# Token products one turn further ahead, between z and y, with a second tile for P

## Chip, core and metric

One core of one Trainium2 chip. The metric is the device time in microseconds (us) of one execution, lower is better; the profiled execution also has a span, from its first to its last instruction.

## What is computed

A residual chain of four conditional layers on x (64 batches x 64 rows x 512):

```python
def _L0(x, W_base, Wt, A, B_w, Wp, scaling, e0):       # e0: one of 4 per batch
    base = einsum('bsi,oi->bso', x, W_base)
    h = einsum('bsi,ji->bsj', x, Wt)
    z = einsum('bsj,brj->bsr', h, A[e0])
    l = einsum('bsr,bor->bso', z, B_w[e0])
    return base + einsum('bso,po->bsp', l, Wp) * scaling[e0][:, None, None]
def _L1(x, W, A, Bm, scalings, e1):                    # e1: one of 8
    return einsum('btd,od->bto', x, W) + einsum('btr,bor->bto', einsum('btd,brd->btr', x, A[e1]), Bm[e1]) * scalings[e1][:, None, None]
x = x + _L0(...)
x = x + _L1(...)
x = x + einsum('bct,bcd->bdt', x, w2[e2])              # e2: one of 8, w2 is 64x64
x = x + einsum('bct,bcd->bdt', x, w3[e3])              # e3: one of 200, w3 is 64x64
```

The first two layers mix the 512 columns and the last two mix the 64 rows of a batch, so the order can be changed.

## The kernel before

The set-up (the first 60 us, in part) builds tables from the weights: `g01` = (1 + W_base)(1 + W) as two parts (a high one and the rest), 4 x 8 pairs of low-rank tables, `v_table` in HBM and `u_tab` in SBUF. The batches are taken two at a time (128 rows, a pair), and four pairs are a turn; there are `QUADS` = 8 turns, i = 0 to 7. For turn i:

- **Tokens** (`token_mix`, line 1019 on): P = (1 + w2)(1 + w3) of each of the 8 batches, 64x64. They read `w2_sel`/`w3_now` (filled by VectorE, `place_w2` and `add_w3`) and write banks 1 and 2 of `y_ps`. The trace shows two instructions for each f32 product, so 16 here. ScalarE copies them to `p_now` (`copy_p`, line 507), the only tile for P.
- **y** (`mix`): x times P, 128 instructions of 64x64 into `y_ps`. VectorE copies y to `y_all` (line 733), ScalarE and VectorE split it into a high part and a rest, `yy` (lines 500 and 740).
- **z** (`reduce`): y times the low-rank table u that GpSimd has placed in `u_sel` (`place_u`, line 408), 64 instructions of 128x32 into bank `o_ps[0]`. ScalarE copies z (line 522).
- **v products** (`add_v`): z times the rows that GpSimd has fetched from `v_table` by indirect DMA (`fetch_v`, line 396), 16 instructions into the four banks `o_ps`.
- **Outputs** (`apply`): `yy` times `g01`, 48 products of 512 columns, added in the same banks. ScalarE copies banks 0 and 2 out (line 532), VectorE 1 and 3 (line 780); SyncE stores.

The order on TensorE is written out by hand. A **burst** of turn i holds what isn't an output: tokens of i+1, z of i, y of i+1 (`mix(i + 1, 1)`, `mix(i + 1, 0)`), v products of i; then come the outputs of i. Bursts 2 to 6 run in a loop (`pe.Fori`, line 1176), burst 1 ahead of it, and turn 7 behind it. In `burst`, the function `x_ready` (lines 1105 to 1108) waits ahead of the last of four chunks of z for p_set (P is copied) and for both loads of x. `next_ready` (1084 on) waits ahead of the last output product for y's copies and for w2 and w3. `v_ready` (1064) waits ahead of the v products. Line 872 is the helper that issues each product, so all products carry its number.

The 64x64 tables of layer 3 come in four picks of 16 batches: GpSimd's `pick_w3(g)` (line 387, indirect DMA, into `v_tab`), SyncE's `spill_w3(g)` to HBM and `load_w3(g)` back into `w3_all`. Picks 2 and 3 (turns 4 to 7) are behind `place_u(2, 1)` in GpSimd's queue. GpSimd's queue of turn 1 is `place_u(1, 1)`, then `fetch_v(1)` after the v products of turn 0.

VectorE's order in turn i: last copy out of i-1, rest of y, the four copies of y(i+1), `place_w2(i + 2)`, `add_w3(i + 2)`, then rests and copies out. Each wait of all this is on a semaphore against a count; in the loop these counts are computed from the loop's register by small sequencer instructions (shown as ALU_OP and FUSED_REGOPS), and a wait that no instruction can carry becomes an EVENT_SEMAPHORE.

## Time and profile before

| | |
|---|---|
| median of 3 runs | 167.16 us (167.01 to 167.16) |
| profiled execution | 168.06 us |
| its span | 166.3 us |
| TensorE busy | 161.5 us, 97% |
| VectorE, GpSimd, ScalarE busy | 55%, 35%, 28% |
| DMA | 30.80 MB, mean 185 GB/s |

The profile's page gives, for the profiled execution, each engine's busy time, the span in 40 slices with the clock that TensorE was granted, and the chain of work that ended last. Behind it stands a trace of single instructions, from which timelines of one engine, busy times in chosen stretches, and the instructions of one line or tile can be read. TensorE has two rows: the products, and the loads of their stationary blocks (PEld). Instructions of a sequencer are marked q. Times are from the span's start.

### The profile page before, as it was taken

Reading aid. Unit: us, or ns where it says so; the run is one execution under the profiler, and the core shown is the slowest. Engines: PE = TensorE matmul, PEld = TensorE weight load, DVE = VectorE, ACT = ScalarE, POOL = GpSimd, SP = SyncE. Lnnn points to the kernel's source line nnn. Section 1 sums busy time; section 2 is a strip of 40 time slices with the busy share of each in tenths; the row PEclk is TensorE's granted clock in tenths of the full one; section 3 lists DMA queues with packets and bytes.
Section 4 is the critical chain, followed back from the end, with each engine's and each line's share of the span. In section 5 each row is a group of like instructions: output and inputs, shape, how many; then the busy total and the mean of one; then the engine's idle time right before and its main releaser. Section 6 shows DMA issues by size and latency. Waiting matters only on the chain.

```text
span 166.3 us, 6376 instructions
## 1 busy us (share of the span) xinstructions
PE 161.5 (97%) x2365; PEld 125.6 (75%) x2365; DVE 92.2 (55%) x220; ACT 47.2 (28%) x90; POOL 57.5 (35%) x167
## 2 busy tenths in 40 slices
PE   5999999999999999999999999999999999999993
PEld 5788738767786868886877887788778886887783
DVE  4856865689877394357726843783484345333011
ACT  3135124573215204220322213122402420422110
POOL 4261120354541269227404820490067007500000
PEclk9999999999999999999999999999999999999999
DMA  4899994658844824569834822683076321433113
GB/s 146 267 371 317 275 267 163 174 210 292 285 149 170 282 102 130 187 181 364 280 132 145 313 96 78 215 289 126 7 269 231 126 91 48 119 126 130 65 63 126
DMA packets 21949, 30.80 MB, mean 185 GB/s; under 512 B 7273, under 2 KB 9705, under 8 KB 21929
## 3 DMA queue, kind: packets, MB, share of 16 engines
q1 hardware_dynamic: 20320, 25.31, 45.7%
q0 software_dynamic: 1600, 5.24, 10.1%
q8 instruction: 10, 0.16, 0.4%
q14 instruction: 11, 0.08, 0.2%
q10 hardware_dynamic: 8, 0.00, 0.0%
HBM read 19.80 MB, written 10.75 MB: 184 GB/s over the span
## 4 chain that ended last, share of the span: by engine, by line
PE 97%; POOL 1%; issue 0%; ACT 0%; POOLq 0%
PE o_ps L872 70%; PE y_ps L872 21%; PE o_ps L917 2%; PE y_ps L956 1%; PE y_ps L885 1%; PE y_ps L925 1%; PE y_ps L931 0%; PE y_ps L969 0%; PE y_ps L1000 0%; ACT o_sb L577 0%; POOL ident L376 0%; POOL piece L373 0%; PE y_ps L934 0%; POOL ident L371 0%; POOL owner L374 0%
## 5 line engine op out<-in xcount | busy, mean ns | idle before, releaser
L872 PE MATMUL o_ps<-g,yy 128*128 128x512 f32 (+1 forms) x384 | 89.0, 389 | 0.0
L872 PEld LDWEIGHTS o_ps<-g,yy 128*128 128x128 f32 x384 | 70.5, 188 | 20.3 <-issue 5.3
L408 POOL COPY u_sel<-u_tab 128x64 f32 x128 | 32.4, 273 | 60.6 <-PE o_ps L872 40.1
L740 DVE TENSOR_TENSOR yy<-y_all,yy 128x512 fp32r<-128x512 f32 x32 | 22.2, 698 | 25.6 <-ACT yy L500 25.4
L500 ACT ACTIVATE yy<-y_all 128x512 fp32r<-128x512 f32 x32 | 20.1, 629 | 51.1 <-PE o_ps L872 23.7
L780 DVE COPY o_sb<-o_ps 128x512 f32<-128x512 f32 x15 | 10.4, 691 | 22.0 <-PE o_ps L872 15.4
L733 DVE COPY y_all<-y_ps 128x512 f32<-128x512 f32 x32 | 19.9, 682 | 3.8 <-PE y_ps L872 3.8
L396 POOL DMA_INDIRECT v_sel<-v_table,v_rows x16 | 15.5, 967 | 10.9 <-PE o_ps L872 7.5
L532 ACT ACTIVATE o_sb<-o_ps 128x512 f32<-128x512 f32 x16 | 9.4, 591 | 21.5 <-PE o_ps L872 17.6
L769 DVE COPY w_sel<-w2T 64x64 f32 x56 | 11.4, 215 | 4.8 <-issue 2.3
L872 PE MATMUL o_ps<-g,wb 128*128 128x512 f32 x48 | 13.4, 424 | 0.0
L872 PE MATMUL y_ps<-p_now,x_odd 64*64 64x64 f32 x768 | 12.6, 220 | 0.0
L872 PEld LDWEIGHTS y_ps<-p_now,x_odd 64*64 64x64 f32 x768 | 11.7, 135 | 0.5
L872 PEld LDWEIGHTS o_ps<-g,wb 128*128 128x128 f32 x48 | 9.0, 199 | 2.8 <-issue 0.8
L872 PE MATMUL o_ps<-v_sel,z 32*64 32x512 f32 (+1 forms) x128 | 8.9, 606 | 0.0
L872 PE MATMUL o_ps<-y_all,u_sel 128*32 128x64 f32 x384 | 7.9, 222 | 0.0
L872 PEld LDWEIGHTS o_ps<-y_all,u_sel 128*32 128x32 f32 x384 | 6.2, 109 | 1.1
L507 ACT ACTIVATE p_now<-y_ps 128x256 f32<-128x256 f32 x6 | 2.3, 385 | 13.7 <-PE y_ps L872 13.7
L917 PE MATMUL o_ps<-ident 128*128 128x128 f32 x12 | 3.0, 425 | 2.1 <-POOL ident L376 2.1
L462 ACT ACTIVATE g<-y_ps 128x512 fp32r<-128x512 f32 (+2 forms) x5 | 2.5, 511 | 8.6 <-PE y_ps L925 7.1
L417 POOL TENSOR_TENSOR wb_sb<-wb_sb,ident 128x128 f32<-128x128 f32 x4 | 1.8, 456 | 8.8 <-DMA wb_sb<-in_L_cond_W_base_dram 8.8
L387 POOL DMA_INDIRECT v_tab<-in_L_cond_weights_dram,spread x4 | 4.3, 1076 | 1.4 <-DVE spread L688 0.8
(121 smaller groups left out, 118.5 us busy)
## 6 DMA issues: line engine op xcount, KB each, us to landing
out_dram<-o_sb SPq DMA_DIRECT2D x14, 512.0 KB
x_odd<-in_x_dram SPq DMA_DIRECT2D x12, 512.0 KB
x_even<-in_x_dram SPq DMA_DIRECT2D x4, 512.0 KB
w_sb<-in_L_cond_W_dram SPq DMA_DIRECT2D x4, 256.0 KB, 5.3
wb_sb<-in_L_cond_W_base_dram SPq DMA_DIRECT2D x4, 256.0 KB, 5.8
wp_sb<-in_L_cond_Wp_dram SPq DMA_DIRECT2D x2, 512.0 KB, 7.8
wt_sb<-in_L_cond_Wt_dram SPq DMA_DIRECT2D x1, 1024.0 KB, 9.9
w_of<-v_tab SPq DMA_DIRECT2D x4, 256.0 KB, 3.2
```

The source lines that it names most:

```text
L387: pool.indirect_dma_start(out=w3_pick[:, g, :], out_offset=None, in_=w3_pieces, in_offset=bass.IndirectOffsetOnAxis(ap=w3_rows[:, g, 0:1], ...
L396: pool.indirect_dma_start(out=v_sel[:, h, :], out_offset=None, in_=v_table, in_offset=bass.IndirectOffsetOnAxis(ap=v_rows[:, h, i:i + 1], ...
L408: nc.gpsimd.tensor_copy(u_sel[2 * h + u][:, :, b, RANK * part:RANK * part + RANK], u_tab[:, :, bass.ds(e, 1), :].rearrange("p k a r -> p k ...
L462: nc.scalar.activation(dst, src, ACT.Copy).then_inc(setup_act, 1)
L500: nc.scalar.activation(yy[u][:, :, 0, :], y_all[u][:, :, :], ACT.Copy).then_inc(yh_set, 1)
L532: nc.scalar.activation(o_sb[:, u, :], o_ps[u][:, :], ACT.Copy).then_inc(o_set, 1)
L733: nc.vector.tensor_copy(y_all[u][:, :, :].rearrange("p k (b t) -> p b k t", b=2), y_of(u)).then_inc(yf_set, 1)
L740: nc.vector.tensor_tensor(yy[u][:, :, 1, :], y_all[u][:, :, :], yy[u][:, :, 0, :].bitcast(F32), ALU.subtract).then_inc(yl_set, 1)
L769: nc.vector.tensor_copy(to[rows, u, :], w2T[rows, bass.ds(g, 1), :].rearrange("p a c -> p (a c)")).then_inc(w2_placed, 1)
L780: nc.vector.tensor_copy(o_sb[:, u, :], o_ps[u][:, :]).then_inc(o_set_dve, 1)
L872: return nc.tensor.matmul(dst, lhsT, rhs, start=start, stop=stop)
L917: nc.tensor.transpose(o_ps[3][:, 0:PART], ident[:, :], ident[:, :])
```

## The change

P of turn i+2 is computed in the burst of turn i. Its tokens stand between z(i) and y(i+1), and are written into banks 1 and 2 of `o_ps` (banks 2 and 3 for turn 2, which is done ahead of y of turn 1). P gets a second tile, `p_next`: ScalarE's `take_p(i + 2)` copies the banks to it after z's copy, and `turn_p(i + 2)` copies `p_next` to `p_now` once y(i+1) has read it. `copy_p` is left for turns 0 and 1. The waits for w2 and w3 of the tokens move from `next_ready` into `x_ready`, with two new ones for the copies out of banks 1 and 2; the wait for u moves to `next_ready`; the v products wait for p_next_set. VectorE places w2 and w3 of turn i+3 in turn i. One more turn is taken out of the loops of TensorE, ScalarE and VectorE. Picks 2 and 3 of w3 move ahead of `place_u(1, 1)`, and SyncE's spills ahead of the first store.

```diff
@@ -148,7 +149,8 @@
         y_ps = ctx.enter_context(nc.psum_tensor("y_ps", [PART, QUAD, D], F32))
-        o_ps = [ctx.enter_context(nc.psum_tensor(f"o_ps{n}", [PART, D], F32)) for n in range(QUAD)]
+        o_all = ctx.enter_context(nc.psum_tensor("o_ps", [PART, QUAD, D], F32))
+        o_ps = [o_all[:, n, :] for n in range(QUAD)]
         bank = [y_ps[:, 0, :], y_ps[:, 1, :], y_ps[:, 2, :], o_ps[2][:, :],
@@ -228,6 +231,10 @@
         p_bank = y_ps[:, 1, 0:QUAD * SEQ]
+        def p_banks(i):
+            return y_ps[:, 1:3, :] if isinstance(i, int) and i < 2 else o_all[:, 2:4, :] if isinstance(i, int) and i == 2 else o_all[:, 1:3, :]
         def crossed(i):
@@ -333,12 +340,12 @@
                 load(3, h)
-            store(0, 0)
-            store(0, 1)
             for g in range(2, PICKS):
                 spill_w3(g)
+            store(0, 0)
             for g in range(2, PICKS):
                 load_w3(g)
+            store(0, 1)
             store(1, 0)
@@ -439,18 +446,17 @@
             fetch_v(0)
+            pool.wait_ge(y_done, 2 * QUAD)
+            for g in range(2, PICKS):
+                pick_w3(g)
             pool.wait_ge(z_done, 2)
             place_u(1, 1)
-            pool.wait_ge(y_done, 2 * QUAD)
             fetch_v(1)
...
                 place_u(i + 1, 1)
-                if i == 1:
-                    for g in range(2, PICKS):
-                        pick_w3(g)
         @block.scalar
@@ -503,13 +509,22 @@
                 wait(act, y_done, QUAD * i)
-                if crossed(i):
-                    nc.scalar.activation(p_now[:, :, :].rearrange("p (v w) d -> p w v d", w=2),
-                                         y_ps[:, 1:3, 0:2 * SEQ].rearrange("p w (v d) -> p w v d", d=SEQ),
-                                         ACT.Copy).then_inc(p_set, 1)
-                else:
-                    nc.scalar.activation(p_now[:, :, :], p_bank.rearrange("p (n d) -> p n d", d=SEQ),
-                                         ACT.Copy).then_inc(p_set, 1)
+                nc.scalar.activation(p_now[:, :, :], p_bank.rearrange("p (n d) -> p n d", d=SEQ),
+                                     ACT.Copy).then_inc(p_set, 1)
+            def take_p(i):
+                act.wait_ge(p_done, 2 * QUAD * (i + 1))
+                act.wait_ge(p_set, i)
+                nc.scalar.activation(p_next[:, :, :].rearrange("p (v w) d -> p w v d", w=2),
+                                     p_banks(i)[:, :, 0:2 * SEQ].rearrange("p w (v d) -> p w v d", d=SEQ),
+                                     ACT.Copy).then_inc(p_next_set, 1)
+            def turn_p(i):
+                act.wait_ge(p_next_set, i - 1)
+                act.wait_ge(y_done, QUAD * i)
+                nc.scalar.activation(p_now[:, :, :], p_next[:, :, :], ACT.Copy).then_inc(p_set, 1)
             def copy_half_z(h):
@@ -531,14 +546,16 @@
                 nc.scalar.activation(o_sb[:, u, :], o_ps[u][:, :], ACT.Copy).then_inc(o_set, 1)
-            def turn(i, more=True):
-                if more:
-                    copy_p(i + 1)
+            def turn(i, ahead=True, more=True):
                 high_y(i, 3)
                 copy_z(i, o_ps[0] if more else y_ps[:, 0, :])
+                if ahead:
+                    take_p(i + 2)
                 if more:
...
                     copy_out(i, 0)
+                    if ahead:
+                        turn_p(i + 2)
                     high_y(i + 1, 1)
@@ -562,14 +579,17 @@
             copy_half_z(1)
+            take_p(2)
+            turn_p(2)
             for u in range(3):
...
             turn(1)
-            with act.Fori(2, QUADS - 1) as i:
+            with act.Fori(2, QUADS - 2) as i:
                 turn(i)
-            turn(QUADS - 1, more=False)
+            turn(QUADS - 2, ahead=False)
+            turn(QUADS - 1, ahead=False, more=False)
             copy_out(QUADS - 1, 0, by=2 * QUAD * QUADS)
@@ -742,7 +762,7 @@
             def add_w3(i, to=w3_now):
-                if isinstance(i, int) and i < 4:
+                if isinstance(i, int):
                     dve.wait_ge(w3_in[i // 2], 16)
@@ -786,8 +806,8 @@
                 if ahead:
-                    place_w2(i + 2)
-                    add_w3(i + 2)
+                    place_w2(i + 3)
+                    add_w3(i + 3)
                 if more:
@@ -836,18 +856,22 @@
                 copy_y(0, u)
-            for u in range(2, QUAD):
-                low_y(0, u)
+            low_y(0, 2)
+            add_w3(2)
             place_w2(2)
+            low_y(0, 3)
             for u in (2, 3, 0, 1):
                 copy_y(1, u)
-            add_w3(2)
-            for u in range(3):
+            for u in range(2):
                 low_y(1, u)
+            place_w2(3)
+            add_w3(3)
+            low_y(1, 2)
             copy_out(0, 1, by=2 * QUAD)
             turn(1)
-            with dve.Fori(2, QUADS - 2) as i:
+            with dve.Fori(2, QUADS - 3) as i:
                 turn(i)
+            turn(QUADS - 3, ahead=False)
             turn(QUADS - 2, ahead=False)
@@ -1025,7 +1049,7 @@
                         rows, to = token_rows(i, u, b), slice(SEQ * b, SEQ * b + SEQ)
-                        out_p = (y_ps[to, 1 + u % 2, SEQ * (u // 2):SEQ * (u // 2) + SEQ] if crossed(i)
+                        out_p = (p_banks(i)[to, u % 2, SEQ * (u // 2):SEQ * (u // 2) + SEQ] if crossed(i)
                                  else p_bank[to, SEQ * u:SEQ * u + SEQ])
@@ -1084,7 +1108,7 @@
                 pe.wait_ge(yf_set, QUAD * i + QUAD)
-                token_ready(i + 1)
+                place_ready(i)
             def reduce(bank, h, ready=None):
@@ -1097,21 +1121,27 @@
                 return done
-            def burst(i):
-                token_mix(i + 1)
-                place_ready(i)
+            def burst(i, ahead=True):
                 pe.wait_ge(o_set, 2 * i - 1)
...
                     pe.wait_ge(p_set, i + 2)
+                    if ahead:
+                        token_ready(i + 2)
+                        pe.wait_ge(o_set_dve, 2 * i - 1)
+                        pe.wait_ge(o_set, 2 * i)
                     for h in range(2):
...
                 reduce(o_ps[0], 1, x_ready).then_inc(z_done, 1)
+                if ahead:
+                    token_mix(i + 2)
                 mix(i + 1, 1)
...
                 v_ready(i)
+                if ahead:
+                    pe.wait_ge(p_next_set, i + 1)
                 add_v(0)
@@ -1163,19 +1193,24 @@
             reduce(y_ps[:, 0, :], 1).then_inc(z_done, 1)
+            token_ready(2)
+            token_mix(2)
             mix_ready(1, 1)
...
             mix(1, 0)
+            pe.wait_ge(p_next_set, 1)
             apply(0, 2, first=True)
...
             burst(1)
-            with pe.Fori(1, QUADS - 2) as i:
+            with pe.Fori(1, QUADS - 3) as i:
                 outputs(i, lambda: next_ready(i + 1))
                 burst(i + 1)
+            outputs(QUADS - 3, lambda: next_ready(QUADS - 2))
+            burst(QUADS - 2, ahead=False)
             outputs(QUADS - 2)
```

## Rows read from the trace of the kernel before

**Rows 1.** the page: busy time of the engines; TensorE's granted clock in 40 slices.

```profile
PE 161.5 (97%) x2365; PEld 125.6 (75%) x2365; DVE 92.2 (55%) x220; ACT 47.2 (28%) x90; POOL 57.5 (35%) x167
...
PEclk9999999999999999999999999999999999999999
```

**Rows 2.** the chain that ended last, in order of time: start us, us, what.

```profile
55.71 1.29 PE o_ps L872 x62
...
86.97 0.39 PE y_ps L872 x16
87.36 1.23 PE o_ps L872 x64
88.59 2.02 PE y_ps L872 x128
...
150.14 1.03 PE y_ps L872 x64
```

**Rows 3.** timeline of 102.2 to 107.5, ScalarE: start, duration us, line, out<-in.

```profile
103.43 0.39 ACT L507 ACTIVATE p_now<-y_ps 128x256 f32<-128x256 f32 x1 [2.24 <-PE y_ps L872]
...
104.52 0.28 ACT L522 ACTIVATE z<-o_ps 128x128 f32<-128x128 f32 x1 [0.19 <-PE o_ps L872]
```

**Rows 4.** stretch, its us, busy us (count) of weight loads from u_sel, clock.

```profile
103.86:104.03 0.17, 0.05 (x4) 1.00 0.00 0
```

**Rows 5.** line 1108 in 103 to 105: duration ns min/median/max, starts us.

```profile
L1108 PEldq ALU_OP  x1: 36/36/36, 103.9 to 103.9; - x1
L1108 PEldq EVENT_SEMAPHORE  x1: 51/51/51, 104.0 to 104.0; - x1
```

**Rows 6.** line 1066, then tile x_odd, 74 to 75: columns as in rows 5.

```profile
L1066 PEldq ALU_OP  x1: 32/32/32, 74.4 to 74.4; - x1
...
L872 PE MATMUL y_ps<-p_now,x_odd x36: 218/218/218, 74.1 to 74.6; 64*64 64x64 f32 x36
```

**Rows 7.** timeline of 37 to 62, VectorE.

```profile
43.22 1.36 DVE L740 TENSOR_TENSOR yy<-y_all,yy 128x512 fp32r<-128x512 f32 x2
44.64 1.33 DVE L769 COPY w_sel<-w2T 64x64 f32 x5
46.43 0.77 DVE L769 COPY w_sel<-w2T 64x64 f32 x3 [0.46 <-issue]
...
49.92 0.41 DVE L753 TENSOR_TENSOR w_now<-w_all,ident 128x256 f32<-128x256 f32 x1
...
52.70 0.68 DVE L780 COPY o_sb<-o_ps 128x512 f32<-128x512 f32 x1
```

**Rows 8.** timeline of 39 to 60.2, TensorE.

```profile
46.29 2.10 PE L872 MATMUL y_ps<-p_now,x_odd 64*64 64x64 f32 x128
...
58.95 1.11 PE L872 MATMUL o_ps<-v_sel,z 32*64 32x512 f32 x16
```

**Rows 9.** timeline of 37 to 68, one ScalarE row, then GpSimd.

```profile
52.66 1.09 ACT L532 ACTIVATE o_sb<-o_ps 128x512 f32<-128x512 f32 x2 [0.61 <-PE o_ps L872]
...
53.38 0.97 POOL L396 DMA_INDIRECT v_sel<-v_table,v_rows  x1 [4.18 <-PE o_ps L872]
54.66 0.94 POOL L396 DMA_INDIRECT v_sel<-v_table,v_rows  x1 [0.30 <-issue]
...
61.06 0.97 POOL L396 DMA_INDIRECT v_sel<-v_table,v_rows  x1 [0.44 <-issue]
62.34 1.07 POOL L396 DMA_INDIRECT v_sel<-v_table,v_rows  x1 [0.30 <-issue]
63.41 1.95 POOL L408 COPY u_sel<-u_tab 128x64 f32 x8
...
66.80 1.21 POOL L387 DMA_INDIRECT v_tab<-in_L_cond_weights_dram,spread  x1 [0.30 <-issue]
```

**Rows 10.** line 396, issues in 53 to 56, then in the whole run.

```profile
DMA to landing us min/median/max: 4.0/4.3/4.6
...
DMA to landing us min/median/max: 3.3/3.7/6.2
```

More of the change, by code:

```diff
@@ L139, in build @@
         p_now = sb("p_now", [PART, QUAD, SEQ])
+        p_next = sb("p_next", [PART, QUAD, SEQ])
         w2_sel = sb("w2_sel", [PART, QUAD, SEQ])
@@ L180, in build @@
         p_done, p_set = sem("p_done"), sem("p_set")
+        p_next_set = sem("p_next_set")
         x_even_in = [sem(f"x_even_in{h}") for h in range(2)]
```

## The prediction, made before the change was run

> **What bounds the kernel now.** I read the page's busy shares first, then the chain that ended last, then the stretches in which the order of TensorE's work changes. TensorE is busy 97% of a 166.3 us span, and its clock stands at the upper level (2.4 GHz) in every slice [rows 1]. The chain is TensorE's own instructions from start to end. So a change counts only by what it takes off TensorE's stream or puts before it. No other engine can give anything back. The chain cuts a turn of the loop into pieces: 0.39 us for 16 token products, 1.23 us for the 64 products of z, 2.02 us for the 128 of y, then the v products and the outputs [rows 2]. Two facts in these pieces matter.
>
> First, the pieces have different shapes, and a change of shape costs. The 128 products of y take 2.02 us with one change of shape behind them, some 14.8 ns each. Sixteen at that pace would be 0.24 us, but the token piece takes 0.39 us: 0.15 us is the change from 64x64 to 128x32 blocks behind it.
>
> Second, the z products take 1.03 us in the last turn, where nothing is waited for within them, but 1.23 us in the loop and 1.29 us in the burst of turn 1 [rows 2]. The cause is the wait before the last chunk. ScalarE copies P from 103.43 for 0.39 us, to 103.82 [rows 3]; TensorE's sequencer then executes its two instructions of line 1108, at 103.9 and 104.0 [rows 5]. Between 103.86 and 104.03 the weight loads were busy for 0.05 us only, finishing old ones [rows 4]. So 0.20 us of a loop turn is P's late copy together with the sequencer's own work behind it.
>
> **Tokens between z and y.** Six sets of token products are moved (turns 2 to 7); one comes ahead of y of turn 1, the others into bursts 1 to 5. z to token is one change of shape, token to y none, as both are 64x64. Each set then costs 16 x 14.8 ns = 0.24 us instead of 0.39 us. Sum: 6 x -0.15 = -0.92 us. This is all on the path.
>
> **The wait for P.** P of the next turn has been in `p_now` since the output of the turn before, so p_set costs nothing now. ScalarE has two copies a turn for one: the second, from SBUF to SBUF, I put at the 0.39 us of the first. Both are covered: after z's copy (0.28 us, ended at 104.80) ScalarE is free until the outputs [rows 3], and the first copy has the whole of y's 2.02 us before the v products overwrite its banks.
>
> But the wait's place stays, and now holds seven waits where it held three: P, w2, w3, two output copies, two loads of x. In the loop their values are computed from the loop's register. The rows show what three cost: two sequencer instructions 0.1 us apart, and 0.18 us from the first to the next weight load (103.86 to 104.03) [rows 4, 5]. I take 0.1 us for an instruction. Against this stands how far the sequencer runs ahead of the array. At the end of y its instruction of line 1066 is at 74.4, and the last product of y, which stands ahead of it in the program, starts at 74.6: a lead of 0.2 us, some 14 pairs of load and product [rows 6]. Seven waits with their values are four instructions (all values shared or fused, two waits in one) to seven (each value by itself). That makes 0.4 to 0.7 us, less the lead 0.2 to 0.5 us of stall, where the loop now has 0.20. I take between five and six instructions, because pairs of waits are already merged at the other places: a stall of 0.33, so +0.13 us in each of the four loop bursts with tokens, +0.52 us (0 to +1.2). Burst 1 waits on constants, which need no computing but do need three instructions: from 0.26 now to about 0.36, +0.10 (-0.25 to +0.3). Burst 6 has no tokens and its waits are long met: -0.20.
>
> A rule of the Trainium skill bears on the lead. "TensorE: Matmul & The Clock Gate", the table at its head, gives TensorE's queue a depth of 64 instructions. By that the lead would be 32 pairs, 0.47 us, and the added waits would be hidden. The row at line 1066 shows less than half of it, so it isn't in the sum.
>
> **One more wait before the v products** (p_next_set). Here a change of shape of 0.15 us hides sequencer work, so +0.01 us each, +0.05 us in all (0 to +0.5). The waits in front of the last output product lie behind products of 512 columns: nothing.
>
> **The start: w2 of turn 2.** TensorE now wants these tokens at 46.29, right behind z [rows 8]. They need all eight w2 copies by VectorE. These now run from 44.64 to about 47.2, of which 46.43 is the start of the last three after a pause of 0.46 [rows 7]. In the new order one `low_y` (0.6 us of spacing) goes behind them and `add_w3` (0.41) comes before; also the code's register load no longer stands behind the `low_y` that waited for ScalarE. So `add_w3` starts at 43.8 and the first copy at about 44.2; eight at 0.29 (five take 1.33 [rows 7]) are done by 46.5 without the pause and by 46.8 with it. Behind TensorE's wait comes 0.1 us of sequencer: it starts between 46.5 and 46.9. I take +0.45 us (+0.15 to +0.7). What is queued behind that wait is y of turn 1 and everything after it.
>
> **The start: v of turn 1.** GpSimd's queue is reordered: both picks of w3 rows now stand before `place_u(1, 1)`, and the fetch of v behind that. The picks wait for all of y(1), which ends about 48.4 + 0.24 + 0.45 = 49.1 (48.4 is 46.29 and its 2.10 [rows 8]). GpSimd begins an indirect DMA 0.72 after its wait (52.66, where ScalarE meets the same wait, to 53.38), the next 1.28 later, and the second of the picks takes 1.21 [rows 9]. So picks at 49.8 and 51.1, ended 52.3; eight u copies right behind, 1.95, to 54.3; 0.44 to the next indirect DMA [rows 9], so v's fetches start at 54.75 and 56.0 instead of 53.38 and 54.66. These two landed after 4.6 and 4.0 us, over the whole run 3.3 to 6.2 with 3.7 in the middle [rows 10]. With 4.0 the second lands at 60.05. The v products start at 58.95 now [rows 8]; by the steps above they want it at 58.95 + 0.24 + 0.45 - 0.15 + 0.10 = 59.6. Before, the fetch landed at 54.66 + 4.0 = 58.7, just in time; so this cover is thin and breaks: +0.50 us (0 to +1.2). `place_u(1, 1)` itself is done at 54.3, more than 1 us before z of turn 1 needs it.
>
> **VectorE and SyncE behind it.** VectorE's copy of bank 1 (52.70 now [rows 7]) moves behind y, two `low_y`, the eight w2 copies, `add_w3` and one more `low_y`: about 48.0 + 2.4 + 1.3 + 2.4 + 0.4 + 0.6, so it ends at 55.8. The new wait for it in burst 1 comes at about 56.7 and is covered by 0.9 us; if that cover goes, what it lacks is paid once. SyncE's first store waits for the same copy and comes some 2.5 us later, the spills and loads of w3 some 13 us earlier. The output buffers are next written in the outputs of turn 1, behind the v products, so nothing waits; the price is contention with the v fetch, inside its range. The w2 and w3 work of VectorE is the same as before in the loop, one turn further ahead. The turn peeled off the loop runs the same products under constants; I cost it at nothing.
>
> **Sum.** -0.92 + 0.52 + 0.10 - 0.20 + 0.05 + 0.45 + 0.50 = +0.50 us. It is made against the profiled execution (168.06 us, of which the span is 166.3); the median of the runs is 0.9 us below that, and since all terms are waits and products within the span I add the sum to the median: 167.16 + 0.50 = 167.7 us.
>
> **Rivals.**
> (A) *The start holds and the sequencer hides most.* If GpSimd's fetch lands after 3.5 us and VectorE has no pause, the two start terms fall from 0.95 to 0.2. If four sequencer instructions do, the loop term is 0. Then -0.92 - 0.2 + 0.1 + 0.05 + 0.2 = -0.8 us: 166.4 us, faster. It decides at a loop piece of z plus tokens under 1.23 + 0.24 us. For it: waits do get merged. Against: the pause and the landing are in the rows as they are.
> (B) *The queue is deeper than the row suggests.* Then the loop's z piece goes to about 1.05 us, -0.18 in each of four turns instead of +0.13: the sum is -0.75 us, 166.4 us with the start's stalls as forecast. The skill's 64 would make it so. Against it: line 1066.
> (C) *They cancel.* One of the two start stalls doesn't come: about 0 us, 167.1 to 167.3.
> (D) *The v fetch meets spills and stores.* With a landing of 5 us, as among the slower half of the range of rows 10, its stall is 1.5 instead of 0.5: +1.5 us in all, 168.7.
> (E) *The wait for P was not the reason of the 0.20 us*, but the sequencer's work alone: then there is no lead to subtract: the loop's stall is 0.53 instead of 0.33, +0.8 us in four turns, and burst 6 gains nothing, +0.2: 168.7.
>
> **Chances.** Forecast 0.38, A 0.17, B 0.08, C 0.20, D 0.08, E 0.09. The range reaches from A and B to D and E: 166.3 to 168.7. About 0.2% (0.33 us) is what a measurement of this kernel can tell from no change. Slower: the forecast's upper four fifths, D and E, 0.48. Within: the rest of the forecast and most of C, 0.26. Faster: A and B and a little of C, 0.26.
>
> **What would show it.** Right: the token piece gone, z 1.3 to 1.4 us in the loop and 1.03 in burst 6, the pieces of y and tokens 2.26 together; a gap on TensorE before the tokens at 46.3 and one before the v products at 59.6. Wrong: a loop piece of z near 1.05 (B), no idle at the start (A, C), or p_set still the last wait of that place. The turn is 15.80 us now; forecast 15.79, A 15.65, B 15.5.

## Result and the profile after

The kernel after the change takes 171.99 us (median of 4 runs, 171.31 to 172.76), the kernel before 167.16 (167.01 to 167.54): a ratio of 1.027, with a 95% interval of 1.025 to 1.030. The forecast was 167.7, in a range of 166.3 to 168.7. The profiled execution took 172.07 us, 170.3 of them span; before it was 168.06 and 166.3.

The page of the kernel after, busy time first, then the queues that carry instructions, then the group of the v products (count | busy us, mean ns | idle before it):

```profile
PE 162.0 (95%) x2365; PEld 124.7 (73%) x2365; DVE 91.1 (53%) x220; ACT 49.8 (29%) x96; POOL 56.7 (33%) x167
...
q8 instruction: 12, 0.20, 0.4%
...
L896 PE MATMUL o_ps<-v_sel,z 32*64 32x512 f32 (+1 forms) x128 | 11.0, 606 | 2.2 <-issue 2.2
```

TensorE did as many products as before [rows 1] in 0.5 us more, so most of the 4 us is idle time. The last row has 2.2 us of it ahead of v products, put down to "issue": time in which TensorE waited for nothing that the profile shows. The kernel before has that group at 8.9 us busy and no idle, and 10 packets (0.16 MB) on q8. The chain of the kernel after shows the places (start us, us, what); these pieces answer to [rows 2]:

```profile
72.15 0.71 PE o_ps L896 x24
72.86 1.90 PE y_ps L896 x127
74.76 1.01 PE o_ps L896 x6
75.77 1.26 issue
77.03 13.13 PE o_ps L896 x114
...
91.06 1.90 PE y_ps L896 x127
92.97 13.11 PE o_ps L896 x120
...
137.99 2.02 PE y_ps L896 x128
140.01 1.00 PE o_ps L896 x3
141.01 0.91 issue
141.92 12.23 PE o_ps L896 x61
154.15 1.03 PE y_ps L896 x64
```

In bursts 2 and 6 TensorE stops some products into the v products. The first six take 1.01 us and are followed by 1.26 us of nothing. Counted from start to start, the v products of burst 2 take 3.37 us and those of burst 6 3.02, where all the others of both kernels take 1.04. That is 2.3 + 2.0 = 4.3 us. Without them the span would be 166.0.

TensorE's timeline around burst 2 shows the rest: z runs from 70.93 to the tokens at 72.40, 1.47 us, with a stall ahead of its last eight products:

```profile
70.93 0.99 PE L896 MATMUL o_ps<-y_all,u_sel 128*32 128x64 f32 x56
72.15 0.32 PE L896 MATMUL o_ps<-y_all,u_sel 128*32 128x64 f32 x8 [0.23 <-issue]
72.40 0.46 PE L896 MATMUL o_ps<-w_now,w_sel 64*64 64x64 f32 x16
72.68 2.08 PE L896 MATMUL y_ps<-p_now,x_odd 64*64 64x64 f32 x128
74.69 1.08 PE L896 MATMUL o_ps<-v_sel,z 32*64 32x512 f32 x6
77.03 1.10 PE L896 MATMUL o_ps<-v_sel,z 32*64 32x512 f32 x10 [1.26 <-issue]
```

At the start stands the wait for w2's copies. The last z product starts at 45.51 and the first token product at 46.11, 0.60 us later where 0.15 is usual; the tokens take 0.28 us, and y(1) starts at 46.39, where [rows 8] have it at 46.29 although this execution was 0.65 us ahead until then:

```profile
46.11 0.46 PE L896 MATMUL o_ps<-w_now,w_sel 64*64 64x64 f32 x16 [0.38 <-DVE w_sel L789]
```

**What stands in the gaps.** The packets of DMA queue q8, "instruction", are 16 KiB each; the built program has 64 bytes an instruction, so one packet is 256 instructions, called a piece here. In the stretch from 74.8 to 74.9 us, at the start of burst 2's v products, one of them starts:

```profile
q8 instruction: 1, 0.02, 59.2%
```

The stretch before (74.7 to 74.8) has none, and the stall ends at 77.03, 2.2 us after the packet's start. In burst 6 a packet starts at 139.57 and the stall ends at 141.92, 2.35 us later. The theory, F from here on: TensorE's program comes in pieces of 256 instructions, the next one is called for when the present one is entered, and a piece that is met for the first time is there only some us later. (Counted in TensorE's rows of the trace, 256 rows back from the end of the stop is 4.3 us earlier for burst 2 and 3.9 for burst 6.) In outputs (48 products, each with its weight load, in 11.1 us, so 115 ns an instruction) 256 instructions last 29 us and nobody notices. In a burst (8 ns an instruction in y: 256 in 2.02 us, [rows 2]) they last 2 us, and TensorE stands still for the rest. That the call is made on entry is argued from these times; no trace shows the call itself. Counted in the built program, the end of a piece lay 16 instructions behind the loop's branch in the kernel before. In the kernel after it lies 21 instructions ahead of the branch, inside the v products, and another two or three products into the v products of the written-out burst 6.

The Trainium skill, "Runtime: NRT & Kernel Launch", section "Instruction fetch mechanics", says that TensorE's instructions come in blocks of 16 KiB (256 instructions), that the next block is fetched while the present one is executed, and that the cost of crossing a boundary is mostly hidden. The trace agrees on the size, and on "mostly": 12 pieces come in the kernel after, and two of them stop TensorE in the bursts. But these two cost 2.3 and 2.0 us.

### The profile page after: what moved, and what is told of

It reads as the page before. It is cut to its first block, busy times and chain, and to the rows that moved or that the text cites. A ratio compares the mean times of both kernels' runs of the same rounds, so it can differ in the third digit from the quotient of the medians.

```text
span 170.3 us, 6372 instructions
## 1 busy us (share of the span) xinstructions
PE 162.0 (95%) x2365; PEld 124.7 (73%) x2365; DVE 91.1 (53%) x220; ACT 49.8 (29%) x96; POOL 56.7 (33%) x167
## 4 chain that ended last, share of the span: by engine, by line
PE 89%; issue 4%; DVE 4%; ACT 1%; DVEq 1%; POOL 1%; POOLq 0%
PE o_ps L896 66%; PE y_ps L896 17%; DVE g L666 1%; PE o_ps L941 1%; PE y_ps L980 1%; PE y_ps L909 1%; PE y_ps L949 1%; DVE v_tab L666 1%; DVEq L789 1%; ACT g L468 0%; PE y_ps L955 0%; DVE w_sel L789 0%; ACT yy L506 0%; DVE yy L760 0%; DVE y_all L753 0%
## 5 line engine op out<-in xcount | busy, mean ns | idle before, releaser
L415 POOL COPY u_sel<-u_tab 128x64 f32 x128 | 31.6, 269 | 59.9 <-PE o_ps L896 42.1
L800 DVE COPY o_sb<-o_ps 128x512 f32<-128x512 f32 x15 | 10.4, 692 | 20.4 <-PE o_ps L896 13.7
L896 PE MATMUL o_ps<-v_sel,z 32*64 32x512 f32 (+1 forms) x128 | 11.0, 606 | 2.2 <-issue 2.2
L896 PE MATMUL o_ps<-g,wb 128*128 128x512 f32 x48 | 12.6, 404 | 0.1
L896 PEld LDWEIGHTS o_ps<-v_sel,z 32*64 32x64 f32 x128 | 2.2, 129 | 5.0 <-issue 4.6
```

Of the source, the lines that this page charges most:

```text
L415: nc.gpsimd.tensor_copy(u_sel[2 * h + u][:, :, b, RANK * part:RANK * part + RANK], u_tab[:, :, bass.ds(e, 1), :].rearrange("p k a r -> p k ...
L800: nc.vector.tensor_copy(o_sb[:, u, :], o_ps[u][:, :]).then_inc(o_set_dve, 1)
L896: return nc.tensor.matmul(dst, lhsT, rhs, start=start, stop=stop)
```

## Experiments

All medians stand against runs of the kernel before on the same chip. The spans are those of the profiled execution. The start of the first output product is given where the set-up, which moves by a microsecond or two from run to run, would hide the difference: the kernel before has 40.04 of 166.3, so 126.3 us from there on, and the kernel after 39.39 of 170.3, so 130.9.

### The kernel before, 32 instructions longer ahead of its loop

```diff
+            for n in range(9):
+                mm(o_ps[3][0:SEQ, 0:SEQ], ident[0:SEQ, 0:SEQ], ident[0:SEQ, 0:SEQ], True, True)
-            keep_warm(9)
+            keep_warm(7)
```

> The kernel before with 9 small f32 products put ahead of the warming transposes and 2 of these left out: 32 TensorE instructions more ahead of the loop, nothing else. Theory F (TensorE's code comes in pieces of 256 instructions, and a piece whose end lies in a burst is awaited for about 2 us): the loop's end now lies 16 instructions behind such an end, as it lies 21 behind in the changed kernel and 16 ahead in the kernel before, so the first run through the loop has a gap of 1.5 to 2.5 us within the v products of burst 2, and the time rises by 1.5 to 2.5 us, to 168.7 to 169.7. Rival R (the v products of burst 2 wait for v rows, z or a bank's copy, which the change made late): nothing of that is changed, no gap, 167.1 to 167.5.

Measured: 170.52 us, ratio 1.019 (1.015 to 1.024), span 168.3. The kernel before, with nothing of the change in it, gets a gap at the same place as the kernel after:

```profile
73.53 2.02 PE y_ps L872 x128
75.56 1.02 PE o_ps L872 x8
76.58 0.15 issue
76.73 12.19 PE o_ps L872 x56
```

The v products of burst 2 take 2.26 us instead of 1.04. From the first output product on the kernel takes 127.8 us, 1.5 more than before, of which this gap is 1.2 and a y(1) longer by 0.22 most of the rest. The median rose by more (2.9): 0.5 us of it is the longer set-up, and the rest is that the profiled executions stand differently to their medians (0.5 below here, 0.9 above in the kernel before). F had the direction and the place right, and rival R, which had no gap, is out. The size was missed: the gap is 1.2 us, not 1.5 to 2.5, and the time lies above the 168.7 to 169.7 expected.

### The kernel after without the warming transposes

```diff
-            keep_warm(9)
...
-            keep_warm(3)
```

> The changed kernel without the 12 warming transposes at the start: 23 TensorE instructions fewer ahead of the loop. F: the whole loop now lies ahead of the piece's end (its branch by 3 instructions), so the gap of 2.3 us in burst 2 goes; the gap of 2.0 us in burst 6 stays but shrinks to 1.0 to 1.6 us, since the end moves to the end of the v products. Set-up costs 0 to 2 us more if TensorE starts at its lower clock. 169.0 to 171.0 in all. R: both gaps stay as they are, and the time is 171.9 or more.

Measured: 171.92 us, ratio 1.024 (1.020 to 1.028). With 23 instructions fewer ahead of the loop's end the gap of burst 2 is gone (v products 1.04), and burst 6's is 1.07 instead of 2.0. Both are as F expected; the time is not (169.0 to 171.0). It did not fall, because the set-up ended 2.4 us later (first output product at 41.78), and because the v products of turn 1 started 1.05 us late. In the set-up eight early products of 512 columns took 3.17 us where the kernel after has 1.85. The granted clock reads 1.00 in both, so why they are slower without the warming transposes stays open. The late v products are a third effect, taken up below.

### The kernel after with its waits taken up before z

```diff
             def next_ready(i, ahead=True):
                 pe.wait_ge(yf_set, QUAD * i + QUAD)
                 place_ready(i)
+                if not isinstance(i, int) or i > 1:
+                    all_ready(i, ahead)    # P, w2, w3, both output copies, x
```

> The changed kernel with the seven waits inside z (P, w2, w3, two output copies, two loads of x) of bursts 2 to 6 moved ahead of the last output product; the number of TensorE instructions is the same. If the sequencer's work on these waits costs the 0.40 to 0.43 us of each loop burst, z falls from 1.44 to 1.47 us to 1.03 us in bursts 2 to 5: -1.7 us, 170.3. If one of these waits was really late (P, w2 or a copy), the stall moves to the last output product and the time stays near 172. F: both gaps in v products stay, within 0.5 us of their 2.3 and 2.0.

Measured: 170.17 us, ratio 1.016 (1.013 to 1.019), span 167.9. The waits now stand ahead of the last output product. z takes 1.03 us in bursts 2 to 5, and the outputs still take 11.1. So seven waits cost nothing behind products of 512 columns and 0.42 us behind products of 16 ns, and none of them was really late. The time is as expected (170.3). Both gaps in the v products stay, but are smaller than F had them: the v products take 2.80 and 2.51 us, so 1.8 and 1.5 us over the usual instead of 2.3 and 2.0.

### The kernel after with its last loop turn back in the loop

```diff
-            with pe.Fori(1, QUADS - 3) as i:
+            with pe.Fori(1, QUADS - 2) as i:
                 outputs(i, lambda: next_ready(i + 1))
                 burst(i + 1)
-            outputs(QUADS - 3, lambda: next_ready(QUADS - 2))
-            burst(QUADS - 2, ahead=False)
```

> The changed kernel with outputs 5 and burst 6 back in the loop of TensorE (and of ScalarE); tokens of a turn 8 are computed that nobody reads. F: burst 6 runs code that is already there: its gap of 2.0 us goes; the tokens cost 0.28 and the longer wait chain 0.4, so 1.3 us less than the changed kernel, 170.7; the gap in burst 2 stays at 2.3 us (same instruction positions). R (something late in data at turn 6): the gap stays, 172.6.

Measured: 171.73 us, ratio 1.023 (1.018 to 1.027). The gap of burst 6 is gone (v products 1.04) and that of burst 2 stays at 3.37. The median does not show the 2 us (170.7 was expected): the span from the first output product on is 130.6, as burst 1's v products started 0.94 us late here and in the kernel after's own trace did not, and z's waits and the tokens of a turn 8 stand in the last burst again.

### The kernel before with its last loop turn written out

```diff
-            with pe.Fori(1, QUADS - 2) as i:
+            with pe.Fori(1, QUADS - 3) as i:
                 outputs(i, lambda: next_ready(i + 1))
                 burst(i + 1)
+            outputs(QUADS - 3, lambda: next_ready(QUADS - 2))
+            burst(QUADS - 2)
```

> The kernel before with one edit: TensorE's loop runs one turn less, and outputs 5 and burst 6 stand once more behind it, with nothing in them changed. The loop's end stays where it was, so no gap in burst 2. F (TensorE stalls where a piece of 256 instructions ends inside a burst and is met for the first time): the written-out burst 6 is code that TensorE has not had yet, and one piece ends some five products into its v products (counted in the built program, as it does two products into them in the kernel after); those v products take 2.5 to 3.1 us instead of 1.04, and the time rises by 1.5 to 2.2 us over the kernel before, 168.7 to 169.5. Rival G (writing a turn out costs nothing; the gap in burst 6 of the kernel after comes from its new order or from P's second tile): v products 1.04 us, 167.2 to 167.6. It also puts a price on the step of the prediction that costed the written-out turn at nothing.

Measured: 169.56 us against 167.63, ratio 1.0125 (1.010 to 1.016). The chain:

```profile
134.79 2.02 PE y_ps L872 x128
136.81 1.00 PE o_ps L872 x5
137.82 0.92 issue
138.74 12.21 PE o_ps L872 x59
```

The gap stands five products into the v products, where the program's count had put it, and costs 2.0 us; a q8 packet starts at 136.25, 2.5 us ahead of its end. The time is 0.06 us above the range expected. This is the price, alone, of the step costed at nothing.

Something else shows here: z in the written-out burst 6 takes 1.04 us, not the 1.23 of the loop, though ScalarE still copies P while it runs. What is gone is the computing of the waits' values from the loop's register.

### The kernel after, 23 instructions shorter

```diff
-            keep_warm(9)
+            for _ in range(2):
+                mm(o_ps[3][:, 0:D], ident[:, :], ident[:, :].unsqueeze(1).to_broadcast([PART, KC, PART]), True, True)
...
-            keep_warm(3)
+            keep_warm(2)
...
                     if ahead:
-                        token_ready(i + 2)
+                        pe.wait_ge(w3_plus, i + 3)
```

> The kernel after with 23 instructions fewer on TensorE ahead of its loop's end: the warming transposes are replaced by two products of 512 columns and two transposes of about the same length, and waits are left out that an earlier wait on the same engine already contains. The order of the work is that of the kernel after. F: the loop's end now lies 2 instructions ahead of the end of a piece instead of 21 behind it, so burst 2's v products take 1.04 us (3.37 in the kernel after), and in burst 6 the end of a piece comes near the last v product, which leaves 0.9 to 1.3 us of the 2.0. With the v fetch of turn 1 anywhere between on time (0) and 1.0 us late, the sum is 172.0 - 2.3 - 0.9 + (0 to 1.0) = 168.8 to 169.8. Rival H (the gap in burst 2 is the new order's own, a wait on P's second tile or on w3's rows): burst 2 stays at 3.4 us and the time at 171.7 to 172.2.

Measured: 169.97 us, ratio 1.016 (1.013 to 1.019), span 167.7. Burst 2's v products take 1.04 us and burst 6's 2.66, so 1.6 us over the usual where 0.9 to 1.3 was expected (the time is 0.2 us above its range): the end of the piece is still met, only nearer to the outputs, two products before the last. Rival H, which had 3.4 us in burst 2, is out. From the first output product on it takes 127.8 us, 3.1 less than the kernel after. z fell too, from 1.44 to 1.47 us to 1.23 to 1.24 in the loop: the trace has four sequencer instructions in it where the kernel after has six, and they follow each other some 0.1 us apart:

```profile
87.52 1.30 PE L903 MATMUL o_ps<-y_all,u_sel 128*32 128x64 f32 x64
88.75 0.46 PE L903 MATMUL o_ps<-w_now,w_sel 64*64 64x64 f32 x16
```

### The kernel after, 32 instructions longer

The same edit as in the first experiment, in the kernel after.

> The kernel after with 32 instructions more on TensorE ahead of its loop (nine small products, two warming transposes fewer). F: the gap of burst 2 follows the number of the instruction, not the work: it moves 32 instructions forward, from the first v products into the last ten y products, and keeps its size (y 4.0 to 4.4 us instead of 2.01, v products 1.04); in burst 6 likewise, y up by 1.8 to 2.3 and v products 1.04. Time 171.9 to 172.9. Rival (the gap belongs to the v products, which wait for z's copy, v's rows or P's second tile): v products of bursts 2 and 6 stay at 3.4 and 3.0 us, y at 2.01.

Measured: 178.06 us, ratio 1.065 (1.061 to 1.069). TensorE's timeline:

```profile
58.80 1.09 PE L896 MATMUL y_ps<-p_now,x_even 64*64 64x64 f32 x61
60.88 1.11 PE L896 MATMUL o_ps<-v_sel,z 32*64 32x512 f32 x14 [0.99 <-issue]
63.05 1.01 PE L896 MATMUL o_ps<-v_sel,z 32*64 32x512 f32 x2 [1.05 <-issue]
63.99 12.78 PE L896 MATMUL o_ps<-g,yy 128*128 128x512 f32 x48
...
78.44 1.93 PE L896 MATMUL y_ps<-p_now,x_odd 64*64 64x64 f32 x119
82.45 0.35 PE L896 MATMUL y_ps<-p_now,x_odd 64*64 64x64 f32 x9 [2.08 <-issue]
82.81 1.12 PE L896 MATMUL o_ps<-v_sel,z 32*64 32x512 f32 x16
```

The gap of burst 2 moved as forecast, to nine products before the end of y: y takes 4.36 us and the v products 1.04. Burst 6 did the same (y 3.86 us). The work at the gap is now y's, whose other products ran on until then, so the gap belongs to the instruction's number. TensorE's rows in the trace (products, weight loads and sequencer instructions; a few can be missing) show it, counted up to the end of each stop:

| kernel, burst | rows ahead | us since the row 256 earlier | us since the packet's start |
|---|---|---|---|
| the kernel after, 2 | 2242 | 4.3 | 2.2 |
| the kernel after, 6 | 4440 | 3.9 | 2.4 |
| 32 longer, 1 | 1729 | 5.0 | 2.3 |
| 32 longer, 2 | 2241 | 4.2 | 2.2 |
| 32 longer, 6 | 4440 | 3.8 | 2.4 |
| waits before z, 2 and 6 | 2242, 4440 | 3.7, 3.4 | 3.0, 3.0 |
| last turn back in the loop, 2 | 2242 | 4.3 | 2.3 |
| the kernel before, 32 longer, 2 | 2241 | 3.1 | 2.3 |
| the kernel before, last turn written out, 6 | 4431 | 3.9 | 2.5 |
| 23 shorter, 6 | 4436 | 3.5 | 2.6 |
| no warming, 6 | 4439 | 3.0 | 2.4 |

In burst 2 the number stays the same, whatever work stands there, and 1729 and 2241 lie 512 apart, two pieces. (Ahead of burst 6 the loop has run three turns, whose length differs by a few rows between these kernels.) What varies is how soon the packet starts, and with it the gap's size; what that depends on stays open.

The time was missed by 5 us, because the shift also put an earlier end (512 instructions, two pieces, before that of burst 2) at the end of burst 1, whose v products had been free of it: they take 3.1 us, behind a late v fetch of 0.99. After these two stops the clock fell. Stretches (us, busy us (count) for PE, weight loads, VectorE, ScalarE, GpSimd, then PEclk, DMA share, GB/s):

```profile
60.00:62.00 2.00, 1.11 (x14) 0.26 (x15) 1.80 (x6) 0.00 (x0) 0.71 (x3) 1.00 1.08 365
62.00:63.90 1.90, 0.85 (x2) 0.13 (x1) 1.10 (x6) 0.00 (x0) 0.00 (x0) 1.00 0.95 218
63.90:67.70 3.80, 3.80 (x10) 2.94 (x10) 0.42 (x1) 0.00 (x0) 3.06 (x9) 0.55 0.73 218
67.70:76.30 8.60, 8.60 (x39) 7.10 (x39) 2.77 (x4) 3.17 (x6) 0.32 (x2) 1.00 0.25 93
```

From 63.9 to 67.7 the granted clock is 0.55, near the lower level of 1.2 GHz, and the outputs of turn 1 take 12.7 us instead of 11.1. So stops in a burst can cost 1.6 us more than themselves. The single stops of burst 2, here and in the kernel after, did not: the clock behind them is 1.00.

### The kernel after with all three taken out

Fewer instructions, no written-out turn, waits early: the edits of three experiments above in one.

> The kernel after with three edits: the 23 instructions fewer, outputs 5 and burst 6 back in the loops of TensorE and ScalarE and VectorE's copies for it (so tokens of a turn 8 are computed from old rows and read by nobody), and the waits of bursts 2 to 6 taken up ahead of the last low product of the outputs before, not in z. F: no gap in burst 2 nor in burst 6, z at 1.03 us. From 172.0: -2.3 (burst 2) -2.0 (burst 6) -2.0 (z, five times 0.4) +0.28 (tokens of turn 8) + (0 to 1.0) (v fetch of turn 1) = 166.0 to 167.0. That is the change without its code: 0.2 to 1.2 us under the kernel before at best. Rival: the three savings overlap, because behind each gap stands another wait (copies on VectorE or ScalarE that the gap gave time to): over 168.

Measured: 168.35 us (12 runs), ratio 1.0041 (1.0021 to 1.0062), span 167.7. Bursts 2 to 6 are clean: z 1.03, tokens 0.28, y 2.03, v products 1.05, outputs 11.11, a turn of 15.50 us against 15.79 [rows 2]. The time expected, 166.0 to 167.0, was missed. What kept it above the kernel before is the stall of turn 1's v rows, the longest of all here:

```profile
57.91 2.08 PE L911 MATMUL y_ps<-p_now,x_even 64*64 64x64 f32 x128
61.73 0.69 PE L911 MATMUL o_ps<-v_sel,z 32*64 32x512 f32 x8 [1.74 <-issue]
```

The second fetch of these rows was issued at 55.55 and landed 6.1 us later. In the seven traces with both of GpSimd's picks ahead of it, this time was 4.4 (the kernel after), 4.7, 5.2, 5.4, 5.5, 5.6 and 6.1 us. In three traces of the old order it was 4.0 (the kernel before), 4.0 and 4.4.

### GpSimd's picks behind the v fetch, then one of them

```diff
+            pool.wait_ge(z_done, 2)
+            place_u(1, 1)
             pool.wait_ge(y_done, 2 * QUAD)
-            for g in range(2, PICKS):
-                pick_w3(g)
-            pool.wait_ge(z_done, 2)
-            place_u(1, 1)
             fetch_v(1)
+            for g in range(2, PICKS):
+                pick_w3(g)
```

> As the kernel with the three edits, and GpSimd's two picks of w3 rows stand behind its v fetch of turn 1 instead of ahead of its last u copies. If the late v rows of turn 1 in three of the four traces with the new order (stalls 0.64 to 0.98 us ahead of burst 1's v products, their rows 5.2 to 5.6 us under way instead of 3.7) come from the picks and from w3's way through DRAM that follows them, the stall goes: 0 to 0.2 us. Against that w3's rows land some 4 us later, at about 67 instead of 62.8, and VectorE, which adds to them ahead of its copies of turn 2, waits as long; its copies are then late for the last outputs of turn 1 if they have less than 4 us of room. On balance 0.7 us less to 1.5 us more than the kernel with the three edits. If the rows are late for the stores' sake alone, the stall stays.

Measured: 170.97 us, ratio 1.019 (1.015 to 1.024). The stall ahead of the v products is gone (0.15 us, the usual step), as expected. But VectorE waited for w3's rows until 71.34, not 67:

```profile
61.62 1.73 DVE L788 COPY w_sel<-w2T 64x64 f32 x8
71.34 0.42 DVE L772 TENSOR_TENSOR w_now<-w_all,ident 128x256 f32<-128x256 f32 x1 [8.00 <-DMA w_all<-w_of]
```

TensorE stood still for 2.34 us ahead of the last output products of turn 1, which took 13.7 us, and its granted clock was 0.62 in the 3.5 us that followed (74.5 to 78.0), so burst 2 ran slower too. The time is 2.6 us above the kernel with three edits, where 0.7 less to 1.5 more was expected. So the stall depends on the picks ahead of the fetch, and their early place is needed.

> The kernel with the three edits (fewer instructions, no written-out turn, waits ahead of z), in which GpSimd picks w3's rows of turns 4 and 5 ahead of the v fetch of turn 1, as the kernel after does, but those of turns 6 and 7 behind it, and SyncE sends them through DRAM behind the first stores. If the late v rows of turn 1 come from the picks and spills that are in flight with them (stall ahead of burst 1's v products 1.96 us with both picks ahead against 0.15, the usual step, with both behind), one pick ahead leaves 0 to 1.0 us, and turn 4's rows still land near 63 to 64, so the outputs of turn 1 keep their 11.1 us (13.7 with both behind). The span from the first output product on was 127.1 us with both ahead; less 1.0 to 1.8 that is 125.3 to 126.1, against 126.3 in the kernel before. Time 166.4 to 167.6. Rival: the rows are late because the fetch itself starts late (it waits for turn 0's v products) and the stores and loads of x fill the queues, whatever the picks do: stall above 1 us, time 168.0 to 168.6.

Here the second pick alone stands behind the fetch. Measured: 168.66 us, ratio 1.006 (1.003 to 1.009), span 166.7; the stall is 1.14 us, against 1.96 with both picks ahead and 0.15 with none. The outputs of turn 1 keep their 11.1. In the median nothing is gained over the kernel with three edits. The 166.4 to 167.6 expected were missed; the stall is above 1 us and the time near 168.0 to 168.6, as the rival had it.

### The kernel before with its waits early

```diff
             def next_ready(i):
                 pe.wait_ge(yf_set, QUAD * i + QUAD)
                 token_ready(i + 1)
+                if not isinstance(i, int) or i > 1:
+                    place_ready(i)
+                    pe.wait_ge(o_set, 2 * i - 1)
+                    for h in range(2):
+                        pe.wait_ge(*x_in(i + 1, h))
```

> The kernel before with one edit: in the loop's bursts the waits for the u rows, for the output bank and for x are taken up ahead of the last low product of the outputs before; only the wait for P stays in z, where the tokens of the same burst make it necessary. The number of instructions does not change. Theory of the prediction (the 0.20 us in z, 1.23 against 1.03, is the copy of P, made after the tokens of the same burst): z stays at 1.23, and the time within 0.3 us of before, 167.3 to 167.9. Rival E (the stall is TensorE's sequencer working through the waits on register values): z falls to 1.03 to 1.10, five bursts gain 0.65 to 1.0 us, 166.7 to 167.0.

Measured: 166.97 us (9 runs) against 167.43, ratio 0.9961 (0.9938 to 0.9983), span 165.3. The burst of turn 3:

```profile
86.62 0.46 PE L872 MATMUL y_ps<-w_now,w_sel 64*64 64x64 f32 x16
87.01 1.10 PE L872 MATMUL o_ps<-y_all,u_sel 128*32 128x64 f32 x64
88.05 2.10 PE L872 MATMUL y_ps<-p_now,x_odd 64*64 64x64 f32 x128
```

With the wait for P still in z, and alone there, z takes 1.03 us. P's copy was never late. The 0.20 us of [rows 2] went with the three waits that were moved, of which only that for x stood within z. x itself was not late either, as the outputs keep their 11.1 us with its wait in them; so it was the sequencer's work on that wait, and the 0.20 us can be had without the change. Rival E of the prediction expected this, 166.7 to 167.0. This is the fastest version measured.

### A tile of its own for turn 0's v rows

```diff
+        v_first = sb("v_first", [PART, 2, D])
...
             fetch_v(0)
+            fetch_v(1)
```

First in the kernel with the three edits, then in the kernel before with early waits.

> The kernel with the three edits, and turn 0's v rows in a tile of their own, so that GpSimd fetches turn 1's right behind turn 0's (at about 47 us) and not when turn 0's v products are done (54.3 and 55.6). Theory (the rows of turn 1 are late because their fetch can only start 7 us ahead of their use, and takes 4 to 6.2 us with GpSimd's 2.5 in front): the stall ahead of burst 1's v products falls from 1.96 us to the usual 0.15, whether w3's picks are in flight or not; the span falls from 167.7 to 165.5 to 166.2, the median by 0.8 to 1.8 us to 166.5 to 167.5. Then what is left of the change against the kernel before with its waits taken up early is the 0.11 us of the tokens in each turn less 0.45 at the start: nothing or a little to either side. Rival (the picks' and spills' traffic delays whatever is on the queues, the earlier fetch as well): turn 0's v products become late, at 52.6 in the kernel with the three edits, by over 0.5 us, and the time stays above 168.

> The kernel before with its waits for u, the bank and x taken up early, and turn 0's v rows in a tile of their own as well. That kernel's trace had a stall of 0.47 us above the usual 0.15 ahead of burst 1's v products (the kernel before's own trace had none). Theory: the stall is gone, and the median falls from 166.97 by 0.2 to 0.6 us to 166.4 to 166.8; it is the fastest of all, since it has neither the later start of turn 2's tokens (0.45) nor any of the new code. Rival: the stall is seldom there and the earlier fetch puts GpSimd's copies of u 2.5 us back: 166.9 to 167.3.

Measured: 169.61 us, ratio 1.011 (1.006 to 1.015), and 171.26 us, ratio 1.015 (1.009 to 1.021). Both missed (166.5 to 167.5 and 166.4 to 166.8 were expected). The stall of turn 1's v rows is gone in both (0.15), so it also depends on how late the fetch starts. But the products ahead of it crawl now. TensorE in y(1) of the second kernel:

```profile
46.33 0.38 PE L875 MATMUL y_ps<-p_now,x_odd 64*64 64x64 f32 x9
47.08 0.34 PE L875 MATMUL y_ps<-p_now,x_odd 64*64 64x64 f32 x3 [0.37 <-issue]
47.87 0.31 PE L875 MATMUL y_ps<-p_now,x_odd 64*64 64x64 f32 x3 [0.44 <-issue]
48.60 0.28 PE L875 MATMUL y_ps<-p_now,x_odd 64*64 64x64 f32 x2 [0.42 <-issue]
49.34 2.90 PE L875 MATMUL y_ps<-p_now,x_odd 64*64 64x64 f32 x111 [0.46 <-issue]
```

Two or three products, then 0.4 us of nothing, four times, while GpSimd issues the added fetch (46.3 to 48.6); y(1) takes 5.8 us instead of 2.0. An estimated 1 us of that is the clock (111 products at the usual 16 ns would take 1.8 us): it is granted at 0.50 from 50.3 to 52.2, behind the stops, and the 111 products take 2.90 us. In the first kernel the clock stays at 1.00, the tokens take 1.2 us instead of 0.28 and y(1) 3.4. No q8 packet starts among these steps. What TensorE lacks in them stays open.

## Why the prediction was wrong

**The chain as TensorE's alone: right**, and with it that only TensorE's stream counts.

**The turn peeled off the loop, "I cost it at nothing": wrong, the largest failed step together with its twin.** It asked what products the turn has, not what its code costs the first time it is run. Written out in the kernel before, it costs 2.0 us (ratio 1.0125). The twin is not in the prediction at all: that new instructions move all that follow. The tokens and waits ahead of the loop's end made the program 37 instructions longer there, and 21 of them lie beyond the end of a piece: 2.3 us in burst 2. Taking 23 away removes the gap, adding 32 moves it into y, and adding 32 to the kernel before makes one, of 1.2 us. 4.3 of the 4.65 us are these two. (4.65 is the difference from the first output product on; the profiled execution of the kernel after happened to reach that product 0.65 us earlier, so its span shows 4.0, while the medians show 4.8.)

**Tokens, -0.92: mis-sized.** A set takes 0.28 us, not 0.24, as the row of burst 2 shows (72.40 to 72.68). That is 6 x -0.11 = -0.66. The change of shape that it saves has its 0.15 us as taken: such a step is still there from z to the tokens, and 0.04 us stands between tokens and y.

**The wait's place, +0.52: mis-sized, and its reason was wrong.** z takes 1.44 to 1.47 us in the loop, not 1.36. The sequencer has six instructions there from 71.51 to 72.04, where between five and six were taken, so +0.9 in four turns. P's late copy had no part in the 0.20 us of the kernel before: its wait alone in z costs nothing. Rival E had the cause right, as the kernel before with early waits shows, but not the size: it gave 1.56 by leaving no lead at all. Rival B, for which the Trainium skill's queue of 64 instructions spoke, is out: seven waits were not hidden.

**Burst 1, +0.10: wrong sign.** z took 1.15 us instead of 1.29 (-0.14). It varies from 1.03 to 1.29 from one kernel to the next. **Burst 6, -0.20: right (1.03), but by luck.** The reason given, that its waits are long met, holds for the loop as well. The kernel before with its last turn written out has 1.04 there too, with P copied as before: what went are the waits' values from the loop's register, and they went with the very step that was costed at nothing. Rival E, which gave burst 6 no gain, missed this. **p_next_set, +0.05: nothing seen.**

**w2 of turn 2, +0.45: right.** The last z product at 45.51, the tokens at 46.11: 0.60 where 0.15 is usual.

**v of turn 1, +0.50: right as a mechanism, absent in the profile shown.** The second pick was quick (0.95 us, not 1.21), the second fetch started at 54.30 instead of 56.0 and landed after 4.4 us, just in time. In six later traces of this order the v products were 0.4 to 1.8 us late, with fetches that took 4.7 to 6.1 us where 4.0 was taken. So it is likely to be part of the medians, nearer to rival D's reason than to the forecast's.

The measured terms are -0.66 + 0.9 - 0.14 - 0.20 + 0.45 + 0 = +0.35 us, near the forecast's +0.50, and +4.3 on top. With the early waits in both, a turn takes 15.50 us with the change and 15.60 without. Those 0.10 us a turn, some 0.5 in all, stand against 0.45 at the start and the late v rows. By these figures the change comes out about even at best, and its best version measured 168.35 us against 166.97 for the kernel before with early waits.

## What to carry to other kernels

Before a change to a stream of very short instructions, count where its 256-instruction pieces end. An end met for the first time inside such a stretch cost 1.1 to 2.3 us here, and any edit ahead of it, a removed wait included, moves it. Code written out of a loop is new code. And take waits on computed values up behind long instructions: what costs 0.2 to 0.4 us between products of 16 ns is free behind 512 columns.

## What the runs showed of the hardware

- Instruction packets of 16 KiB: 10 in the kernels whose bursts 2 to 6 run in the loop, 12 in those with a written-out turn. In the kernel after none starts between 77 and 126 us, the later turns of the loop: the code of a loop turn (some 560 instructions) was not fetched again.
- Where TensorE stopped at the end of a piece, it went on 3.0 to 5.0 us after the instruction 256 rows earlier (12 stops in eight kernels), and 2.2 to 3.0 us after the packet's start.
- Between products of 16 ns, the sequencer instructions of waits on register values cost TensorE 0.20 us (two, and in another kernel four) and 0.41 to 0.44 us (six), though no wait was late. Behind products of 512 columns nine cost nothing.
- The second indirect fetch of v rows of turn 1 landed after 4.4 to 6.1 us in seven kernels with GpSimd's picks ahead of it, and after 4.0 to 4.4 us in three without.
- Behind a burst with stops of 0.99 and 1.05 us the granted clock was 0.55 for 3.8 us, and behind one stop of 2.34 us among the outputs 0.62 for 3.5 us. Behind single stops of 1.26 and 2.08 us in a burst it stayed at 1.00.
